# A selective-SSM block on one core: all of u's products ahead of both exponents' products in TensorE's slot

## The reference, cut to what matters

```
xs, z = split(h @ in_w); xs = silu(xs); proj = xs @ xproj_w
dt = softplus(proj[:, :512] + dt_bias); Bm, Cm = proj[:, 512:576], proj[:, 576:]
A = -exp(A_log)                                   # 512 channels x 64 states
hst = hst * exp(dt_t[:, None] * A) + (dt_t * x_t)[:, None] * B_t[None, :]
y_t = einsum('ds,s->d', hst, C_t)
```

## Time and profile before

| | us |
|---|---|
| median of 3 runs | 5366.41 |
| lowest and highest | 5361.21, 5369.36 |
| the profiled execution | 5370.79 |
| its span | 5369.1 |

### The profile page before, as it was taken

How to read it: one execution, slowest core, us unless ns; L and a number is a source line. 1 busy time by engine, 2 the same in 40 slices (tenths; PEclk the granted TensorE clock), 3 DMA queues, 4 the chain that set the end, 5 groups by cost and what they waited for, 6 DMA issues and landing times. The chain is left out here.

```text
span 5369.1 us, 130492 instructions
## 1 busy us (share of the span) xinstructions
PE 4970.5 (93%) x44784; PEld 2522.5 (47%) x44784; DVE 4726.2 (88%) x2419; ACT 3415.8 (64%) x11498; POOL 3751.7 (70%) x6613
## 2 busy tenths in 40 slices
PE   6999999999999999999999999999999999886898
PEld 4444444444444444444444444444444444443444
DVE  2999999999999999999999999999999999996443
ACT  4666766666666766666676766666676766663112
POOL 4777768677777868777776868677776868674211
PEclk8999999999999999999999999999999999998899
DMA  3121111111121111112121111111121211113441
GB/s 106 38 64 43 54 48 52 54 39 61 38 64 42 55 48 52 55 38 61 38 64 43 61 41 52 55 37 61 39 63 39 64 38 43 36 29 104 146 153 66
DMA packets 433144, 306.75 MB, mean 57 GB/s; under 512 B 215920, under 2 KB 336240, under 8 KB 432496
## 3 DMA queue, kind: packets, MB, share of 16 engines
q1 hardware_dynamic: 428272, 294.39, 18.2%
q10 hardware_dynamic: 4224, 4.19, 0.2%
HBM read 187.27 MB, written 111.15 MB: 56 GB/s over the span
## 5 line engine op out<-in xcount | busy, mean ns | idle before, releaser
L891 DVE TENSOR_TENSOR_SCAN b_hs<-b_dA,b_u 128x1024 f32<-128x1024 f32 x2048 | 4540.7, 2270 | 273.9 <-ACT b_u L818 187.0
L1056 PE MATMUL b_ex<-b_dd,b_aw 32*128 32x512 f32 x8192 | 2710.1, 642 | 33.7 <-POOL b_dd L534 15.4
L1043 PE MATMUL b_u<-b_ud,b_bw 32*128 32x256 f32 x16384 | 2336.5, 401 | 258.9 <-DVE b_hs L891 237.6
L800 ACT ACTIVATE b_dA<-b_ex 128x496 f32<-128x496 f32 x4096 | 2289.7, 589 | 145.4 <-PE b_ex L1056 142.6
L1043 PEld LDWEIGHTS b_u<-b_ud,b_bw 32*128 32x128 f32 x16384 | 1425.9, 184 | 1119.1 <-issue 635.5
L1075 PE MATMUL b_y<-b_hs,b_cw 128*32 128x256 f32 x16384 | 1309.9, 390 | 2.3 <-DVE b_hs L891 2.3
L818 ACT ACTIVATE b_u<-b_hin 128x32 f32<-128x32 f32 x1792 | 364.7, 203 | 1192.2 <-PE b_u L1043 1006.9
L534 POOL TENSOR_TENSOR b_dd<-b_dr,b_mask 128x512 f32<-128x512 f32 x1024 | 1073.2, 1048 | 52.2 <-DVE b_hs L891 39.4
L543 POOL TENSOR_TENSOR b_ud<-b_ur,b_mask 128x512 f32<-128x512 f32 x1024 | 1083.5, 1058 | 0.0
L1056 PEld LDWEIGHTS b_ex<-b_dd,b_aw 32*128 32x128 f32 x8192 | 856.6, 183 | 106.7 <-ACT b_dA L800 65.9
L570 POOL TENSOR_TENSOR b_hm<-b_first,b_hs 128x32 f32<-128x32 f32 x1792 | 480.1, 268 | 539.4 <-ACT b_first L799 517.8
(11 more groups left out here) (104 smaller groups left out, 2283.1 us busy)
## 6 DMA issues: line engine op xcount, KB each, us to landing
b_u<-scratch_ut SPq DMA_DIRECT2D x256, 128.0 KB, 2.9
scratch_y<-b_ysb SPq DMA_DIRECT2D x128, 256.0 KB, 2.3
scratch_xs<-b_xs SPq DMA_DIRECT2D x64, 256.0 KB, 2.4
scratch_sz<-b_sd SPq DMA_DIRECT2D x64, 256.0 KB, 2.2
scratch_dt<-b_sd SPq DMA_DIRECT2D x64, 256.0 KB, 2.1
scratch_ut<-b_uT SPq DMA_DIRECT2D x64, 256.0 KB, 2.4
b_ur<-scratch_ut SPq DMA_DIRECT2D x1024, 16.0 KB
b_dr<-scratch_dt SPq DMA_DIRECT2D x1024, 16.0 KB, 1.7
```

Of the source, the lines that this page charges most:

```text
L800: nc.scalar.activation(dA[:, j % NDA, h, :, 1:TC], src[:, :, 1:TC], ACT.Exp).then_inc(exp_done, 1)
L891: nc.vector.tensor_tensor_scan(hs[:, v, :, :, kp].rearrange("p d t -> p (d t)"), dA[:, j % NDA, :, :, :].rearrange("p h d t -> p (h d t)") ...
L1043: ins = nc.tensor.matmul(dst[:, :, tb, :], bw[row(r), c % 2, tb, :], ud[row(r), j // 2 % NPR, tb, :, :], start=(tb == 0), stop=(tb == NTB ...
L1056: nc.tensor.matmul(e[bank_of[what]][:, :], aw[row(r), p % DIRS, v, :, :].rearrange("p b s -> p (b s)"), dd[row(r), (p * PAIRS + j // 2) % ...
```

## The change

In `step` the two exponents' products leave their places behind each token block's products of u. The four products of u now come first, in the order in which they had stood, and both exponents' products come behind them. Nothing is added or removed, and no wait is changed in itself; the bank wait of each exponent's product moves with it.

```
                     for tb in range(NTB):
                         for h in range(2):
                             inject(p, j, h, tb)
-                        if then:
-                            exponent(*then, tb)
+                    if then:
+                        for h in range(2):
+                            exponent(*then, h)
```

## The result

The changed kernel takes 5331.93 us (median of 4 runs, 5331.09 to 5336.34), the kernel before on the same chip 5366.46 us (4 runs, 5361.21 to 5369.36). The ratio is 0.9938, with a 95% interval of 0.9921 to 0.9956: 34.5 us less. The profiled execution took 5332.06 us with a span of 5330.4, so 38.7 less than that of before.

A forecast was written before the change was run, and what follows sets the result against it. VectorE's scan bounds the kernel, so only its 273.9 us of idle time, mostly ended by ScalarE's carry, can be won. 23 + 8 = 31 us off gives 5340 profiled, 5335 us as median, range 5320 to 5357.

The forecast's parts named there:

- The mechanism: TensorE's products signal in program order, so u's signals and ScalarE's carry wait behind the first exponent's; carry 0.05 us earlier per slot.
- Parts one to three: Slots with side jobs: earlier u signals 1.3, late exponents freed 0.4, costs -0.2; net 1.5 us a pass, 23 us in all.
- Part two: Slots like 53 and 37 to 39: an exponent late for its bank no longer holds the carry; about 0.4 us a pass.
- Part three: First chunk of a pass: the exponent's signal comes 0.08 later behind u's two; with GpSimd's chain, -0.2 us a pass.
- Part four: Turns of x, slots 112 and 116: u no longer waits behind the exponent's bank; 1.08 us in seven passes, 7.6 us.
- the exponents do not start later: Rival, every TensorE slot: exponents can't pass u's products and start with u's last records; 5816 us or more, 4%.
- the exponents' signal doesn't count: Rival: the chain of 20 waits hangs on the first half's exp, not the carry, each losing 0.08; 5390 us, 4%.
- the next limit: Rival: GpSimd's `hin` or TensorE's chain takes back the carry's earlier time; no effect within 0.2%, 5356 to 5377 us, 12%.

The follow-up runs named there:

- the waiting carry: Changed kernel's TensorE order, but ScalarE's carry also waits for the first exponent's product of its slot: 5365.84 us, ratio 0.9998 to the kernel before.
- the exponent between: Against the kernel before, the first exponent's product stands before the very last product of u instead of before the last two: 5361.86 us, ratio 0.9990.
- the exponent first: Against the kernel before, the first exponent's product and its bank wait stand ahead of all four products of u, the second last: 5397.23 us, ratio 1.0059.
- one signal in the old order: Kernel before, products in their order, but only u's last product signals and ScalarE and VectorE wait for that alone: 5342.98 us, ratio 0.9954.
- the wait ahead: Changed kernel's order of products, but the first exponent's bank wait stands ahead of all four products of u: 5370.58 us, ratio 1.0010 to the kernel before.
- the last with one signal: Repeat of the changed kernel with one signal for u and one wait on each of ScalarE and VectorE: 5314.04 us, ratio 0.9895 to the kernel before.
- the first group: Runs of the unchanged kernel on one chip beside the waiting carry, the exponent between, the exponent first and the turns alone: median 5367.16 us.
- the two kernels which divide signal and wait: Changed kernel with both of u's signals but only the later waited for, 5322.01 us; or with one signal that each engine waits for twice, 5322.38 us.

## Why the prediction was right, and where its sizes were off

It said 5335 and the kernel takes 5332. The mechanism is the one it named: the kernel whose carry waits for the exponent again gave all of the gain back. To size its terms, here are the times from the first scan of a pass to that of the next, in us, read from the starts of the scans in the profiled executions (passes counted from 1):

| passes | before | after | difference |
|---|---|---|---|
| 2, 4, 6, 8, 10, 12, 14, 15 (no turns) | 299.9 to 300.4 | 298.2 to 298.7 | -1.6 or -1.7 each |
| 3, 7, 9, 11 (turns) | 302.6, 302.4, 302.5, 303.2 | 300.1, 300.0, 299.8, 300.5 | -2.5, -2.4, -2.6, -2.7 |
| 1, 5 (turns) | 305.7, 305.1 | 300.4, 300.3 | -5.3, -4.7 |
| 13 (turns) | 302.3 | 301.4 | -0.9 |

- **Parts one to three** were 1.5 us a pass and are 1.67: 25 us instead of 23. The idle time before the scans should fall to about 243 and fell to 242.5; the carry of slot 36 should begin 1.29 after the start and begins 1.28 after it. The kernel with the new order in the turns alone leaves 23 us for these parts.
- **Part two** went as written: ScalarE's second half in slot 53 begins 0.26 earlier (0.21 to 0.26 were given), and slot 55's wait is 0.25 shorter (0.20 and 0.05). Only the carry is earlier than thought, by 0.50 from the slot's start instead of about 0.3: ScalarE, the bound I had named, came to it sooner in the slot. The scans of the part didn't depend on it.
- **Part three**: the exp of the first chunk begins 0.16 after the exponent's end instead of 0.10, so 0.06 later where 0.08 was said, and the wait before slot 8's scan grew by 0.08, as said, from 0.48 (1640.75 in DVE's timeline of before) to 0.56. Slot 6 and the scans from slot 8 on, ACT's and DVE's timelines of the changed kernel, against the earlier trace rows:

```profile
1618.16 0.59 PE L1056 MATMUL b_ex<-b_dd,b_aw 32*128 32x512 f32 x2
...
1618.91 1.06 ACT L800 ACTIVATE b_dA<-b_ex 128x496 f32<-128x496 f32 x2 [0.54 <-PE b_ex L1056]
...
1624.10 17.73 DVE L891 TENSOR_TENSOR_SCAN b_hs<-b_dA,b_u 128x1024 f32<-128x1024 f32 x8 [0.56 <-PE b_y L1075]
```

- **Part four**: a pair of turns was to bring 1.08, 0.60 in the first turn and 0.48 in the second. In the third pass the idle time of the first went from 1.32 to 0.68, 0.64 less, and that of the second from 1.14 to 0.70, 0.44 less: 1.08 together, as said. In the passes' length less of it arrives. Over the four passes of the table's second line the turns are worth 2.58 - 1.67 = 0.9 each, so 6.4 us instead of 7.6; in the kernel with the turns alone five such passes are 0.9 to 1.1 shorter.
- **What was not in the sum** is TensorE's clock. Its granted level in the main phase is 2.4 GHz (1.00 in the windows), and in the turns of passes 1 and 5 of the kernel before it fell to 1.2 GHz for a few us (0.50 in the window from 380 to 384). The windows view of before, of the changed kernel in the like place, and of its one pass that does show it (us, then busy time and instructions of PE, PEld, DVE, ACT, POOL, granted clock, DMA share, GB/s):

```profile
380.00:400.00 20.00, 18.06 (x166) 8.48 (x164) 16.97 (x8) 12.73 (x46) 12.12 (x26) 0.87 0.12 35
```

```profile
380.00:400.00 20.00, 17.42 (x184) 8.62 (x184) 19.25 (x10) 14.03 (x51) 13.70 (x28) 1.00 0.11 35
3970.00:3990.00 20.00, 18.14 (x184) 8.87 (x181) 17.06 (x8) 13.13 (x49) 13.62 (x28) 0.96 0.11 34
```

The stretches don't hold quite the same slots, but both with a fall have 8 scans where the undisturbed one has 10. The scan that such a fall delays, in the kernel before and in the thirteenth pass of the changed kernel, in DVE's timelines:

```profile
380.59 2.29 DVE L891 TENSOR_TENSOR_SCAN b_hs<-b_dA,b_u 128x1024 f32<-128x1024 f32 x1 [2.10 <-ACT b_u L818]
```

```profile
3972.19 8.82 DVE L891 TENSOR_TENSOR_SCAN b_hs<-b_dA,b_u 128x1024 f32<-128x1024 f32 x4 [2.27 <-ACT b_u L818]
```

2.10 and 2.27 of idle stand where 1.32 and 0.68 are usual. Against a turn's usual gain (2.58) the two passes of before give 2.7 + 2.2 = 4.9 more, and the one of the changed kernel takes 1.7 back: 3 us beyond the sum. With 25 and 6.4 that is 34.6 in the 15 passes. The other 4 of the 38.7 lie ahead of the first scan (108.24 against 107.45) and behind the last one, and another execution of the changed kernel doesn't confirm them. Its second profiled one takes the same time as the first from the first scan to the last (106.3 to 4873.6 against 107.4 to 4874.8), but its span is 2.1 longer (5332.5 against 5330.4), and behind the last scan it takes as long as before.

Whether the clock's part is luck can be told from the other traces. In six of them something of the first exponent, its product, its signal or its bank wait, can still hold u or the carry in the turns, as before: there a window over a turn shows a fall in 2 of 7 turns (before), 3 (the waiting carry), 1 (the exponent between), 4 (the exponent first), 1 (one signal in the old order) and 7 (the wait ahead), 18 of 42. In the seven with the new order in the turns and a free carry it is 1 of 7 in two traces (the changed kernel and the last with one signal) and none in the other five, 2 of 49. So the falls go with an exponent that can hold u or the carry, and having fewer of them looks like a gain of the change that the prediction left out. It isn't shown beyond these counts, since each trace is a single execution. The runs' mean granted clocks agree. Of the 27 runs of before in the first group, the eight with 0.987 take 5370.5 us on average, the nine with 0.988 take 5367.9 and the ten with 0.989 take 5364.4. The kernel with the turns alone fits too: it won 11.5 where 6.4 to 7.6 were due. What in a turn makes the clock fall, the rows don't tell.

The forecast isn't close because large errors cancelled: parts one to three came out 2 us larger, part four 1 us smaller, and the 3 us of the clock were in no term. Parts one, two and three were measured only together, so errors among them could have cancelled.

Of the rivals, the exponents do not start later (0.02 after u's first record), the exponents' signal doesn't count except in the first chunk, and the next limit didn't take the carry's earlier time back.

Of the expectations, that of one signal in the old order was 3 us short, for the wait that it left out. That of the two kernels which divide signal and wait had named the outcome, 5322, as its middle case. The one that failed in sign was that of the exponent ahead of u, and its error was in the prediction's picture as well: I had taken a bank wait as free as long as the bank is free. It has a price by itself in front of a slot's first product (slot 20), and it makes all that stands behind it late when the bank is. The change kept the bank waits behind u's first product, so the prediction didn't suffer from it.

## What to carry to other kernels

Where products of several row groups share TensorE, look at which product's signal is on the critical chain, and put everything that may wait, with its own waits, behind that product in the program: a late product holds the signals of all that stand behind it even when these have long run. Then signal once, with the last product, and let each engine wait once; a satisfied wait and an unneeded signal each cost the chain some 0.02 us a slot here, together two thirds of what the reordering brought. Look at the waits in front of a loop's first instruction too: one more, behind three others, cost 0.11 us in each such slot here, and behind a single one nothing.

## What the runs showed of the hardware that I had not expected

- A product behind a late one on other row groups runs but cannot tell: in the kernel with the exponent between u's last two products, u's records end at 1740.61 and the carry begins at 1741.19, 0.16 after the exponent's end. Starts are free of this order: the exponent behind four products of u begins 0.02 after the first of them.
- One wait more in front of an even slot's first product lengthens TensorE's idle time from 0.25 to 0.36 us in slot 20, with the scan still the last thing waited for, whether the exponent's product or u's is the first. In odd slots, with two waits fewer, the gap stays as it was. The bank wait moved there costs 38 us in all, part of it in turns in which the clock fell.
- A wait that is already met, on ScalarE and on VectorE, costs nearly as much as one signal of TensorE: 11 us for either by the medians, 19 to 22 for both, the carry 0.02 and 0.04 earlier.
- The granted clock fell in single turns of x (0.87 over 20 us in pass 1 of before), in 18 of 42 turns where the exponent could hold the carry and in 2 of 49 where it could not, and cost 1.7 to 2.7 us in each of the three turns that were sized.
